# Mixing channels ahead of the cosine transform in a fused residual-convolution kernel

## The reference

```
x1 = relu(conv3x3_dilated2(x, w1) + b1)
x2 = relu(conv3x3_dilated2([x, x1], w2) + b2)
x3 = relu(conv3x3_dilated2([x, x1, x2], w3) + b3)
x4 = relu(conv3x3_dilated2([x, x1, x2, x3], w4) + b4)
fea = relu([x, x1, x2, x3, x4])                  # 160 channels
fea = einsum('ij,bcjk,lk->bcil', H, fea, H)      # cosine transform of rows and columns
y   = conv3x3(fea, w6) + b6 + x                  # 160 channels to 32
```

## Time and profile before

| | |
|---|---|
| runs | 517.45 us median (516.25 to 519.08) |
| profiled execution | 518.84 us, its span 516.9 us |
| granted TensorE clock, mean | 0.921 |
| PE, DVE, ACT, POOL busy | 434.0, 415.7, 206.8, 37.9 us |
| steps 1 to 7 | from 43.9 to 382.05 us |
| transform of the last pair | to 410.6 us |
| quantised block | to 516.9 us |

### The profile page before, as it was taken

How to read it: one execution, slowest core, us unless ns; L and a number is a source line. 1 busy time by engine, 2 the same in 40 slices (tenths; PEclk the granted TensorE clock), 3 DMA queues, 4 the chain that set the end, 5 groups by cost and what they waited for, 6 DMA issues and landing times. The chain is left out here.

```text
span 516.9 us, 6137 instructions
## 1 busy us (share of the span) xinstructions
PE 434.0 (84%) x1930; PEld 292.6 (57%) x1932; DVE 415.7 (80%) x766; ACT 206.8 (40%) x281; POOL 37.9 (7%) x32
## 2 busy tenths in 40 slices
PE   1977879887997999799879988996987566599977
PEld 1745657675775667676757775675755222244422
DVE  7387588878977996799699779967898789779766
ACT  4222451254136124512541372254135379166640
POOL 5020020002000200020020002000000200011000
PEclk9988989898999899899989988998898869699969
DMA  6323144023412231333234122212313000000004
GB/s 209 107 62 98 42 85 126 21 55 85 108 40 61 59 108 40 78 68 92 54 85 114 38 62 59 60 41 59 79 42 72 7 1 0 0 1 0 0 1 162
DMA packets 16708, 32.08 MB, mean 62 GB/s; under 512 B 3120, under 2 KB 10416, under 8 KB 16688
## 3 DMA queue, kind: packets, MB, share of 16 engines
q1 hardware_dynamic: 16688, 31.82, 24.8%
HBM read 9.20 MB, written 2.10 MB: 22 GB/s over the span
## 5 line engine op out<-in xcount | busy, mean ns | idle before, releaser
L640 PE MATMUL conv_ps<-D,w_hl 128*128 128x512 f32 x576 | 151.7, 419 | 14.4 <-DVE w_hl L536 10.4
L640 PEld LDWEIGHTS conv_ps<-D,w_hl 128*128 128x128 f32 x576 | 112.6, 197 | 49.5 <-issue 13.8
L744 PE MATMUL z_ps<-E,mix_hl 128*96 128x512 f32 x270 | 77.5, 449 | 20.3 <-DVE E L418 20.3
L744 PEld LDWEIGHTS z_ps<-E,mix_hl 128*96 128x96 f32 x270 | 50.1, 188 | 46.0 <-DVE E L418 23.5
L287 ACT ACTIVATE r<-conv_ps,bias_sb 64x512 f32<-64x512 f32 x32 | 21.9, 684 | 99.6 <-PE conv_ps L640 99.2
L398 DVE STREAM_TRANSPOSE T<-r 64x256 f32<-64x256 f32 x128 | 55.7, 435 | 1.7
L282 ACT ACTIVATE r<-r 64x512 f32<-64x512 f32 x32 | 20.2, 631 | 79.1 <-DVE r L385 79.1
L418 DVE TENSOR_TENSOR E<-z_ps,E 32x256 fp32r<-32x256 f32 x60 | 35.8, 597 | 17.3 <-ACT E L308 16.6
L719 PE MATMUL e_ps<-hc,T 128*128 128x128 f32 x240 | 34.8, 306 | 16.0 <-DVE E L418 14.3
L1098 PE MATMUL ps<-q_q,q_diag 128*128 128x512 bf16 x192 | 46.2, 403 | 1.5 <-DVE q_q L1011 1.5
L372 DVE CAST D<-r 64x512 fp32r<-64x512 f32 x48 | 20.1, 419 | 33.9 <-ACT r L287 27.9
(11 more groups left out here) (118 smaller groups left out, 474.0 us busy)
## 6 DMA issues: line engine op xcount, KB each, us to landing
D<-D SPq DMA_DIRECT2D x96, 126.0 KB, 2.3
E<-E SPq DMA_DIRECT2D x32, 248.0 KB, 3.5
x_own<-in_x_pads SPq DMA_DIRECT2D x16, 288.0 KB, 3.5
xb<-in_x_res SPq DMA_DIRECT2D x8, 256.0 KB, 2.8
out<-q_res SPq DMA_DIRECT2D x8, 256.0 KB, 2.0
w_raw<-in_w_conv SPq DMA_DIRECT2D x6, 192.0 KB, 4.1
w_raw<-in_w_int SPq DMA_DIRECT2D x1, 843.0 KB, 4.4
mix_raw<-in_w_mix SPq DMA_DIRECT2D x1, 192.0 KB, 3.6
```

What stands on the lines that cost most here:

```text
L640: last = nc.tensor.matmul(conv_ps[u][:, bank, :], w_hl[:, wp, n, d, :], D[f][u][:, xp, :, 2 * d:2 * d + S], start=start and d == 0 and h == 0,
L744: nc.tensor.matmul(z[0:96, k, :], mix_hl[:, wp, d, :], E[u][:, xp, 16 * k + d:16 * k + d + 16, :], start=d == 0 and h == 0, stop=False, sk ...
```

## The change

The channels are mixed first, over the untransformed pixels, and the nine taps' mixed values are transformed afterwards.

- SyncE gathers the features of an image into `F` (32 channels each of x, x1, x2, x3 on 128 partitions): x from a new input `x_mix`, the others from the ReLU's output `r`, two DMAs for each feature and image. They stand in its queue ahead of the same feature's halos. `r` is one buffer per image now, no longer one per feature. The shifts of E4 are gone.
- ScalarE and VectorE make the halves of F (`high_f`, `low_f`) and of x4 (`high_4`, `low_4`, into `X4`, 96 partitions); GpSimd copies the high half of x4 onto a third group of partitions (`copy4`).
- TensorE mixes with the pixels as weights and the mixing matrix as moving operand (`mix_rows`, `mix_x4`): 8 groups of 128 pixels, 4 matmuls of 288 columns each (9 taps x 32 channels). Groups go round four PSUM banks; ScalarE takes each out into `Y` (`take_mix`).
- Stage 1 is 36 fp32 matmuls of 256 columns an image, each in a 32x32 tile: four groups of rows (the pixels' partitions) times three groups of columns (dy), summed over three dx. Each row group has its own PSUM bank. VectorE turns this out of PSUM with `turn_s1`, which reads across the four banks. Stage 3 is unchanged in size.
- `turn`, `low_e`, `evac_e` and the line 404 are gone.
- The order on TensorE: conv0 of both, conv1 of both, mix 0, conv2 of image 0, stage 1 of image 0, conv2 of image 1, mix 1, stage 1 of image 1, conv3 of both, stage 3 of both.

The core of the diff:

```diff
@@ sync
+            def gather(s, f, u):
+                sp.wait_ge(relu_done[u], s * 3 + f)
+                for h in range(2):
+                    sp.dma_start(F[u][32 * f:32 * f + 32, h],
+                                 r[u][32 * h:32 * h + 32].rearrange("p a b l -> p (a b l)")).then_inc(f_in[u], 16)
...
+                for u in range(2):
+                    gather_x(s, u)
+                    gather(s, 1, u)
+                    halos(s, 1, u)
...
+                for f in (2, 3):
+                    for u in range(2):
+                        gather(s, f, u)
+                        halos(s, f, u)
@@ gpsimd
+            def copy4(s):
+                pool.wait_ge(x_split[1], min(s + 2, PAIRS))
+                for u in range(2):
+                    pool.wait_ge(x4_hi[u], s + 1)
+                    for h in range(2):
+                        nc.gpsimd.tensor_copy(X4[u][64:96, h],
+                                              X4[u][32 * h:32 * h + 32, h].bitcast(F32)).then_inc(x4_copied[u], 1)
+                        pool.wait_ge(x4_copied[u], 2 * s + h + 1)
@@ scalar
+            def high_f(s, u):
+                act.wait_ge(f0_in[u], s * 16 + 16)
+                act.wait_ge(f_in[u], s * 96 + 96)
...
+                nc.scalar.activation(F_hl[u][:, 0], F[u][:], ACT.Relu).then_inc(f_hi[u], 1)
+            def high_4(s, u):
+                act.wait_ge(added[u], s * 2 + 2)
...
+                for h in range(2):
+                    k = slice(32 * h, 32 * h + 32)
+                    last = nc.scalar.activation(X4[u][k, h], r[u][k].rearrange("p a b l -> p (a b l)"), ACT.Relu)
+                last.then_inc(x4_hi[u], 1)
+            def take_mix(p, u):
+                n = p * 2 + u
+                act.wait_ge(s1_done, n + GRANT)
+                for g in range(8):
+                    act.wait_ge(y_done, n * 8 + g + 1)
+                    nc.scalar.activation(Y[:, g], mix_bank(p, u, g), ACT.Copy).then_inc(y_out, 1)
...
+                take_part(s, 2, 1)
+                relu(s, 2, 1)
                 if not is_first(s):
+                    take_mix(p, 0)
+                if not no_next(s):
+                    high_x(s + 1, 1 - odd, batch + 2)
+                relu(s, 3, 0)
+                relu(s, 3, 1)
                 if not is_first(s):
+                    take_mix(p, 1)
+                high_f(s, 0)
+                high_f(s, 1)
+                take_part(s, 4, 0)
+                take_part(s, 4, 1)
+                high_4(s, 0)
+                high_4(s, 1)
@@ vector
+            def low_f(s, u):
+                dve.wait_ge(f_hi[u], s + 1)
+                nc.vector.scalar_tensor_tensor(out=F_hl[u][:, 1], in0=F[u][:], scalar=0.0,
+                                               in1=F_hl[u][:, 0].bitcast(F32), op0=ALU.max,
+                                               op1=ALU.subtract).then_inc(f_lo[u], 1)
+            def low_4(s, u):
+                dve.wait_ge(x4_hi[u], s + 1)
+                for h in range(2):
+                    k, low = slice(32 * h, 32 * h + 32), slice(32 - 32 * h, 64 - 32 * h)
+                    last = nc.vector.scalar_tensor_tensor(
+                        out=X4[u][low, h], in0=r[u][k].rearrange("p a b l -> p (a b l)"), scalar=0.0,
+                        in1=X4[u][k, h].bitcast(F32), op0=ALU.max, op1=ALU.subtract)
+                last.then_inc(x4_lo[u], 1)
+            def turn_s1(p, u):
...
+                nc.vector.transpose(
+                    Zt[:, u, :].rearrange("p (o l) -> p o l", l=S),
+                    banks(p, u)[0:96, :, 0:PX // 4].rearrange("p j (g o) -> p o g j", o=C)).then_inc(zt_done, 1)
...
+                low_f(s, 0)
                 if not is_first(s):
+                    turn_s1(p, 1)
+                add_parts(s, 4, 0)
+                add_parts(s, 4, 1)
+                low_4(s, 0)
+                low_4(s, 1)
+                low_f(s, 1)
@@ tensor
+            def mix_rows(p, u, g):
+                h, k = g // 4, slice(NP * (g % 4), NP * (g % 4) + NP)
+                if g >= 4:
+                    pe.wait_ge(y_out, (p * 2 + u) * 8 + (g - 3))
+                elif g >= 2 and not u and not is_before_last(p):
+                    pe.wait_ge(added[g - 2], p * 2 + 3)
+                y = mix_bank(p, u, g)
+                for n, (wp, xp) in enumerate(((0, 0), (0, 1), (1, 0))):
+                    nc.tensor.matmul(y, F_hl[u][:, xp, h, k], mix_hl[:, wp],
+                                     start=n == 0, stop=False, skip_group_check=True)
+            def stage1(p, u):
+                n = p * 2 + u
+                pe.wait_ge(y_out, n * 8 + 8)
+                pe.sem_inc(s1_begun, 1)
+                out = banks(p, u)
+                for d in range(3):
+                    for j in range(4):
+                        k = slice(32 * j, 32 * j + 32)
+                        for dy in range(3):
+                            at = 96 * d + 32 * dy
+                            last = nc.tensor.matmul(out[32 * dy:32 * dy + 32, j, 0:PX // 4], hc[k, d],
+                                                    Y[k, :, at:at + 32], start=d == 0, stop=d == 2,
+                                                    skip_group_check=True)
+                last.then_inc(s1_done, 1)
```

More of the change, by code:

```diff
@@ L703, in conv3, with mix_ready, mix_x4_ready @@
                 conv_alone(s, u, 4, 5)
+            def mix_ready(p, u):
+                pe.wait_ge(f_lo[u], p + 1)
+                if banks(p, u) is sums_ps:
+                    for v in range(2):
+                        pe.wait_ge(added[v], 2 * PAIRS)
+                else:
+                    pe.wait_ge(zt_done, p * 2 + (u + GRANT))
+                    pe.wait_ge(st_done, p * 2 + GRANT)
+            def mix_x4_ready(p, u):
+                pe.wait_ge(x4_lo[u], p + 1)
+                pe.wait_ge(x4_copied[u], p * 2 + 2)
@@ L705, in stage1, with mix_x4, mix @@
+            def mix_x4(p, u, g):
+                nc.tensor.matmul(mix_bank(p, u, g), X4[u][:, g // 4, NP * (g % 4):NP * (g % 4) + NP],
+                                 mix4_hl[:], start=False, stop=True, skip_group_check=True).then_inc(y_done, 1)
+            def mix(p, u):
+                mix_ready(p, u)
+                mix_x4_ready(p, u)
+                for g in range(8):
+                    mix_rows(p, u, g)
+                    mix_x4(p, u, g)
             def stage1(p, u):
                 n = p * 2 + u
-                pe.wait_ge(turned[u], p * 5 + 5)
@@ L766, in step @@
                 dct = not is_first(s)
[L767 to L769 removed]
+                if is_last(s):
+                    mix_ready(p, 0)
+                    for g in range(4):
+                        mix_rows(p, 0, g)
+                    mix_x4_ready(p, 0)
+                    for g in range(4):
+                        mix_x4(p, 0, g)
+                    for g in range(4, 8):
+                        mix_rows(p, 0, g)
+                        mix_x4(p, 0, g)
+                    mix_ready(p, 1)
+                    mix_x4_ready(p, 1)
+                    for g in range(4):
+                        mix_rows(p, 1, g)
+                        mix_x4(p, 1, g)
+                    stage1(p, 0)
+                    for g in range(4, 8):
+                        mix_rows(p, 1, g)
+                        mix_x4(p, 1, g)
+                    stage3(p, 0)
+                    stage1(p, 1)
+                    stage3(p, 1)
+                    return
+                conv0(s, 0)
+                conv0(s, 1)
                 if is_second(s):
```

451 lines of the change are left out of this document (145 added, 306 removed).

## The result

The changed kernel takes 455.18 us (median of 4 runs, 453.53 to 456.17) beside 517.52 for the kernel before on the same chip, a ratio of 0.879 [0.875, 0.883]. The forecast was 482 in a range of 453 to 507. The time is inside, but near the low end, where the PE-bound rival (458) stood.

What follows compares the result with a forecast made beforehand. The prediction took PE to bound the step, VectorE holding it up in two places. Start 42.9 + seven steps 301.0 + quantisation 2.5 + tail 28.5 = 374.9 against 410.6: 35.7 us less, so 482 us (range 453 to 507).

Steps and rivals of the forecast that it cites:

- PE-bound rival: Rival, chance 0.24: turn_s1 takes 1.25 us, GpSimd's copies hide, PE's work sets the step at 40.0 us; 458 us.
- The mechanism: Step's end: VectorE's serial work from image 1's mixing to the halo makes PE wait 2.2 us; period 41.3 us.
- E: Point in a step where image 1's mixing ends on PE; the halo was forecast to land 17.8 us later.
- GpSimd's share: Delay of VectorE at low_4 by GpSimd's four copies of x4: 1.7 us a step, ends 0 and 5.0.
- The clock term: Behind PE's new halo wait the clock falls to half for one stretch: 1.7 us added a step, giving 43.0.
- The chain: VectorE's order from E: low_f(0), turn_s1(1), additions, low_4, low_f(1), split, then halo: 17.8 us a step.
- The rest of the loop: PE from the halo's landing to the next E: conv matmuls, both mixings, conv2, stage 1: 23.5 us a step.
- Step 0: The start before the seven steps, with its chain of ReLU, split and halo unchanged: 42.9 us instead of 43.9.
- The tail: Behind the seven steps: PE's first mixing needs low_f(1) and both turn_back on VectorE; 28.5 us, as today.
- heavy VectorE tail: Rival, chance 0.16: turn_s1 2.4 us, copies 1.1, evacuations 0.6; period 46.1 us with the clock, 505 us.
- The serial case: Rival, chance 0.08: stage 1's row groups stream one after another, 5.95 us an image; slower than before, 534 us.
- The signs named: Trace signs: stage 1's twelve starts, 288-column pace, PE's 2.2 us halo wait, turn_s1's mean, copies alternating with low_4.

Runs made afterwards that it cites:

- chain1: Changed kernel with one spare copy of low_f(1) on VectorE ahead of the real one; 466.03 us, 0.906 of the kernel before.
- s3_out: Changed kernel with stage 3 reading Zt in runs of eight values and writing PSUM in steps of 128 bytes; 455.74 us, 0.880.
- rowgroups: Changed kernel with stage 1's loop over the four row groups put outermost, same 36 matmuls; 473.89 us, 0.917.
- chain3: Changed kernel with three spare copies of low_f(1) on VectorE ahead of the real one; 491.95 us, 0.955.
- nocopy: Changed kernel with GpSimd's copy4 copying only 8 of 512 columns, the rest zero; 448.90 us, 0.871.

## Why the prediction was right, and where it missed

**The mechanism** stands. It put the end of the step at VectorE's chain from image 1's mixing to the halo. chain1 (1.15 us a step for one more instruction) and s3_out (0.84 us off PE, nothing off the step) each show it for the part from the additions on. Its first part, high_f, low_f(0) and turn_s1, did not bind: it was done 0.45 us before the additions could start, and the path up to them ran over stage 1 and conv3 (rowgroups). Counted from E (195.92), the steps of the chain against the forecast:

| | forecast | measured |
|---|---|---|
| low_f(0) done | 3.2 | 2.8 |
| turn_s1(1) done | 4.8 | 4.1 |
| first addition starts | 4.8 | 4.5 |
| four additions done | 7.6 | 7.3 |
| low_4 with GpSimd's share done | 12.2 | 11.5 |
| low_f(1) done | 13.5 | 12.8 |
| split done | 14.9 | 13.8 |
| halo landed, PE goes on | 17.8 | 17.1 |
| PE ready for it | 15.6 | 16.6 |
| from there to the next E | 23.5 | 22.6 |

**What went wrong is sizes.** The 27.1 us between 483.1 and 456.0 are these, to within half a microsecond:
- The clock term, "I add 1.7 a step": 11.9 us in seven steps, and none of it came. It rested on a wait of 2.2 us "as long as those after which it now falls"; the wait was 0.5, and one of 1.6 brought it in none of steps 3 to 7 of chain1. Of all steps only step 1 has such a stretch. Its price was too high as well: 1.2 in chain3, 0.84 between steps 4 and 3 of the kernel before. The forecast read the grant of 0.96 as one stretch, rightly, but took its waits from a step with two (0.93).
- The chain, 0.7 a step, 5.1 us. turn_s1 took 1.244 us and not 1.6: reading PSUM with steps of a bank costs nothing beside the 1.246 in line, though for this step only the 0.3 us by which the additions start sooner count. GpSimd's share was 1.3, not 1.7. The halo landed 3.3 us behind the split where 2.9 stood, but low_f(1) and the split took 0.4 less. The evacuation took 412 ns, not 500, near the low end of its bounds.
- The rest of the loop, 0.9 a step, 6.5 us. Mixing took 0.134 a matmul ((195.40 - 192.18) / 24), below even the low end of 0.138, so 4.3 us for image 1 where 4.7 stood, and 4.5 for image 0 where 5.3 stood with its wait of 0.6.
- Against these, steps 1 and 2 are 2.8 and 0.9 us over the others, where 2.5 stood for step 1 and nothing for step 2: 1 us back.
- Step 0, 1.6 us, and the quantised part, 2.6: the change leaves it alone, and its granted clock was 0.89 in place of 0.85. The tail was forecast at 28.5 and took 28.4.

**Two terms hid each other.** PE's work was forecast at 37.8 us a step, and 23.6 + 8.6 + 3.7 + 1.8 = 37.7 is what the pace of its parts gives. But the mixing was 0.8 too dear and stage 3 0.5 too cheap: "stage 3 is unchanged in size" was taken for "unchanged in time", though the diff changes the order in which Zt lies.

**Stage 1** is right: twelve tiles at work within 0.15 us, 1.84 us an image for the forecast 1.75, where 5.95 had been the other end. The Trainium skill (TensorE: Matmul & The Clock Gate, Part 3: Packing small matmuls) states that row and column tiles compose; the trace now agrees for four by three. rowgroups shows how much of it hangs on the order of the program, 3.01 us in another.

**GpSimd and VectorE.** low_4 goes from 689 ns to 1021 beside the copies (866 ns each). The Trainium skill (SBUF — State Buffer, SBUF: two separate sides) has an exclusive lock held for a whole instruction; that the four of each engine alternate agrees. But the 2.4 us that the forecast worked out from it did not come: low_4 is 1.3 us longer for four copies. So each copy holds VectorE up for 0.33 us, less than the lowest price in the forecast (0.44). How long a copy takes by itself was not measured, so whether VectorE stands for the whole of it stays open.

**The rivals.** The PE-bound rival had the nearest time, but not the cause: with PE as the limit, chain1 would have cost little and s3_out would have gained. It lies just beneath, as nocopy shows (step 39.0 once the chain is 1.3 us shorter). Its two premises, turn_s1 at 1.25 and copies that hide, were half right. The heavy VectorE tail failed on turn_s1 and the evacuations. The serial case did not happen, and its price of 5.95 was never reached: the worst order tried gave 3.01, below the 4.9 from which it would have decided.

**The signs named** were the right ones, except the bound on the period: "wrong if under 39.5" was passed by 39.6, with two terms off by 12 and 6.5 us.

## What to carry to other kernels

When two engines' chains close a loop within a microsecond of each other, find the one that binds by adding one spare instruction and reading the step, not the share of busy time; then look for the engine's own waits inside that chain, for where it stands idle another path comes in (here stage 1 and conv3, ahead of the additions), and count what lies behind the last of them as one: moving low_f(1) inside it gained nothing here. A clock term that hangs on a wait should be weighed by the chance of that wait, not added to it whole: here it alone was 12 of the 27 us. "Unchanged" in a diff has to be checked for layout as well as for size.

## What the runs showed of the hardware

- An fp32 matmul of 256 columns whose moving operand is read with steps of 128 bytes passes in 0.43 us in place of 0.24 (stage 3, 1.84 us for both images against 1.00). Runs of 32 bytes, and steps of 128 bytes on the side of PSUM, cost nothing (s3_out). For VectorE's transpose of 96x1024 it is the other way about: PSUM read with steps of a bank is free (1244 ns to 1246), SBUF written with steps of 128 bytes is not (2034).
- Matmuls of different row groups ran side by side when they alternated in the program (72 records in 1.84 us), and only in part when the nine of one group stood together (3.01 us).
- Waits of PE of 1.5 to 1.6 us left the clock at its high level (chain1, steps 3 to 7), those of 3.8 to 4.4 never did (chain3, steps 2 to 7). Those of 1.8 to 2.1 us in the kernel before were followed by the low level six times in eight, one of 1.8 in s3_out was too, and one of 2.13 in chain1 was not.
